# Second layer's gathered experts: the token table in 32 operations, values in two, turned rows and weighing on ScalarE

## What is computed

```python
x_flat = x.reshape(n, c)
scores = (x_flat @ Wg.T).T
top_vals, token_idx = jax.lax.top_k(scores, capacity)
token_w = jax.nn.softmax(top_vals, axis=-1)
xg = x_flat[token_idx]
h = silu(einsum('eic,ehc->eih', xg, W1)) * einsum('eic,ehc->eih', xg, W3)
y = einsum('eih,ech->eic', h, W2) * token_w[..., None]
out = zeros_like(x_flat).at[token_idx.reshape(-1)].add(y.reshape(-1, c))
```

## Time and profile before

| | |
|---|---|
| runs | 2541.8, 2552.1, 2556.6 us |
| profiled execution | 2541.7 us, span 2539.8 |
| busy, share of the span | PE 81%, weight loads 54%, DVE 57%, ACT 42%, POOL 25% |
| the phase of the change | about 1176 to 1336 us of the span |
| its POOL DMAs | 32 gathers 47.4 us busy, 32 scatters 53.5 |
| its tables (`place`) on DVE | 8, together 36.0 us busy |

### The profile page before, as it was taken

One profiled execution on the slowest core, in us unless ns is written; L12 is line 12 of the kernel. 1 busy time (PEld: TensorE's weight loads), 2 busy tenths in 40 slices (PEclk: granted clock), 3 DMA queues, 4 the chain that ended last, 5 costly groups with the idle time before them and its releaser, 6 DMA issues. The chain is left out here.

```text
span 2539.8 us, 42804 instructions
## 1 busy us (share of the span) xinstructions
PE 2055.0 (81%) x16323; PEld 1362.3 (54%) x16323; DVE 1440.6 (57%) x3407; ACT 1068.7 (42%) x2525; POOL 627.8 (25%) x680
## 2 busy tenths in 40 slices
PE   5989999977699993665545678582899999999798
PEld 3546666566566772223324344462566666666565
DVE  2037777534544444555626998014467776777577
ACT  4236556512434442230106534233466666666322
POOL 3018800021200001001674000406233333333100
PEclk9989999978699996675775656695799999999999
DMA  2070110020000003000135001211000000000000
GB/s 60 17 43 5 13 24 2 2 61 16 34 8 1 1 1 116 0 0 9 27 39 176 1 19 35 84 52 50 22 1 1 1 1 1 1 1 1 1 18 17
DMA packets 110168, 61.11 MB, mean 24 GB/s; under 512 B 65272, under 2 KB 104720, under 8 KB 108816
## 3 DMA queue, kind: packets, MB, share of 16 engines
q1 hardware_dynamic: 101568, 49.60, 8.6%
q0 software_dynamic: 7680, 8.40, 1.8%
q10 hardware_dynamic: 720, 0.40, 0.1%
HBM read 36.87 MB, written 21.50 MB: 23 GB/s over the span
## 5 line engine op out<-in xcount | busy, mean ns | idle before, releaser
L2749 ACT ACTIVATE l_prob<-l_ps,l_neg_max 128x128 f32<-128x128 f32 (+1 forms) x512 | 208.2, 419 | 45.6 <-DVE l_neg_max L2809 40.7
L1468 ACT ACTIVATE l0a_prob<-l0a_pst 128x1024 f32<-128x1024 f32 x128 | 131.0, 1024 | 119.9 <-PE l0a_pst L1386 119.9
L2634 POOL TENSOR_TENSOR l_prob<-l_prob,l_total 128x256 f32<-128x256 f32 x128 | 78.4, 612 | 371.9 <-DVE l_total L2817 371.9
L1519 DVE TENSOR_REDUCE l0a_peak<-l0a_ps 128x4 f32<-128x1024 f32 x128 | 156.2, 1221 | 15.8 <-PE l0a_ps L1381 13.7
L2805 DVE TENSOR_TENSOR l_ps<-l_ps,future 128x512 f32<-128x512 f32 x128 | 89.4, 698 | 108.6 <-PE l_ps L2680 108.6
L1381 PE MATMUL l0a_ps<-l0a_k,l0a_q 32*128 32x256 f32 x1024 | 146.3, 405 | 3.3 <-ACT l0a_prob L1468 2.5
L474 ACT ACTIVATE l0e_hidden<-l0e_ph,l0f_b 128x512 f32<-128x512 f32 x128 | 88.0, 687 | 141.1 <-PE l0e_ph L389 141.1
L1386 PE MATMUL l0a_pst<-l0a_q,l0a_k 32*128 32x256 f32 x1024 | 145.8, 400 | 0.2 <-ACT l0a_prob L1468 0.2
L399 PEld LDWEIGHTS l0e_py<-l0f_w,l0e_hidden 128*128 128x128 f32 x1024 | 119.6, 192 | 36.0 <-ACT l0e_hidden L474 32.0
L389 PE MATMUL l0e_ph<-l0f_h_ch,l0f_w 128*128 128x512 f32 x256 | 125.0, 603 | 11.9 <-PEq L43 11.9
L2635 POOL TENSOR_TENSOR l_prob<-l_prob,l_total 128x512 f32<-128x512 f32 x128 | 133.0, 1039 | 0.0
(11 more groups left out here) (481 smaller groups left out, 4949.5 us busy)
## 6 DMA issues: line engine op xcount, KB each, us to landing
l_band<-zero SPq DMA_DIRECT2D x16, 272.0 KB, 3.5
x_tok<-in_x_dram SPq DMA_DIRECT2D x2, 2048.0 KB, 8.0
l2f_w<-in_L_ffn_w_dram SPq DMA_DIRECT2D x2, 2048.0 KB, 9.8
l_rows<-l_band SPq DMA_DIRECT2D x16, 256.0 KB, 3.5
l1f_w<-in_L_ffn_W_dram SPq DMA_DIRECT2D x3, 1024.0 KB, 7.1
gd_tri<-gp_tri SPq DMA_DIRECT2D x8, 256.0 KB, 2.0
l0f_w<-gd_tri SPq DMA_DIRECT2D x8, 256.0 KB, 12.9
gd_tri<-l0f_w SPq DMA_DIRECT2D x8, 256.0 KB, 8.8
```

Source lines behind the costliest of these rows:

```text
L1468: act.activation(prob[:, (n // 2) % 2, pair, :, :].rearrange("p g t s -> p g (t s)"), pst[:, :, :, :].rearrange("p g t s -> p g (t s)"), A ...
L1519: dve.tensor_reduce(to, ps[m % 2][:, :, :, :], AX.X, ALU.max, negate=True).then_inc(max_ready, 1)
L2749: act.activation(prob[:, m % 4, h, cols], ps[m % 2][:, h, cols], ACT.Exp, bias=neg_max[:, m % 4, h, t:t + 1], accum_out=total[:, m % 4, h, ...
```

## The change

The table `place` is made in 32 operations, one for each block, with the lane as a scalar per partition and one streamed input. The five value operations become two, of 2 and 3 values. `save_xt` and `weigh` move from VectorE to ScalarE, the weighing as four operations with the weight as scale. VectorE's order in each turn of the loop becomes `find(e+2)`, both gates, `build(e+3)`; ScalarE's `save_xt(e)`, first Silu, `weigh(e-1)`, second Silu. TensorE, GpSimd and SyncE stay as they are.

```diff
             @block.scalar
             def _(act):
                 act.wait_ge(*ready)
-                for u in range(E * chunks):
+
+                def save_xt(e):
+                    act.wait_ge(turned, e + 1)
+                    if e >= 2:
+                        act.wait_ge(h3_ready, chunks * (e - 1))
+                    act.activation(xt[:, e % 2, :], pt[:, :, :].rearrange("p b t -> p (b t)"), ACT.Copy).then_inc(xt_saved, 1)
+
+                def open_gate(u):
                     act.wait_ge(h1_ready, u + 1)
                     if u >= 2:
                         act.wait_ge(hidden_ready, u - 1)
                     act.activation(act_out[:, u % 2, :], ph1[u % 2][:, :], ACT.Silu).then_inc(act_ready, 1)
+
+                def weigh(e):
+                    act.wait_ge(y_ready, e + 1)
+                    if e >= 2:
+                        act.wait_ge(scattered, 16 * GB * (e - 1))
+                    act.wait_ge(found_ready, e + 1)
+                    for j in range(GB):
+                        ins = act.activation(y[:, e % 2, j, :], py[:, j, :], ACT.Copy, scale=weight[:, e, j:j + 1])
+                    ins.then_inc(y_saved, 1)
+
+                for e in range(E + 1):
+                    if e < E:
+                        save_xt(e)
+                        open_gate(chunks * e)
+                    if e >= 1:
+                        weigh(e - 1)
+                    if e < E:
+                        open_gate(chunks * e + 1)
...
                     link(dve.tensor_tensor(mark[:, e % 2, :, :], r.high[:, e, :].unsqueeze(2).to_broadcast(wide),
                                            r.quarter[:, :].unsqueeze(1).to_broadcast(wide), ALU.is_equal))
-                    for v in range(V):
-                        value = r.number[:, :, v] if v < 2 else r.piece[:, e, :, v - 2]
-                        dve.tensor_tensor(what[:, e % 2, :, :, v], mark[:, e % 2, :, :], value.unsqueeze(2).to_broadcast(wide), ALU.mult)
-                    full = [P, BLK, P]
-                    dve.tensor_tensor(place[:, e % 2, :, :], r.lane[:, e, :].unsqueeze(2).to_broadcast(full),
-                                      r.column[:, :].unsqueeze(1).to_broadcast(full), ALU.is_equal).then_inc(built, 1)
+                    for first, values in ((0, r.number[:, :, :]), (2, r.piece[:, e, :, :])):
+                        n = values.shape[-1]
+                        dve.tensor_tensor(what[:, e % 2, :, :, first:first + n], mark[:, e % 2, :, :].unsqueeze(3).to_broadcast([P, BLK, GB, n]),
+                                          values.unsqueeze(2).to_broadcast([P, BLK, GB, n]), ALU.mult)
+                    for b in range(BLK):
+                        ins = dve.tensor_scalar(place[:, e % 2, b, :], r.column[:, :], r.lane[:, e, b:b + 1], None, ALU.is_equal)
+                    ins.then_inc(built, 1)
...
                 build(0)
                 build(1)
                 find(0)
                 find(1)
                 build(2)
-                for e in range(E + 1):
-                    if e < E:
-                        save_xt(e)
+                for e in range(E):
                     if e + 2 < E:
                         find(e + 2)
-                    if e < E:
-                        gate(chunks * e)
-                    if e >= 1:
-                        weigh(e - 1)
+                    gate(chunks * e)
+                    gate(chunks * e + 1)
                     if e + 3 < E:
                         build(e + 3)
-                    if e < E:
-                        gate(chunks * e + 1)
```

More of the change, by code:

```diff
@@ L2078, in find @@
                        .then_inc(token_ready, 1)
[L2080 to L2084, removed]
                 def gate(u):
@@ L2092, in gate @@
                     dve.tensor_tensor(hidden[:, e % 2, f, :], ph3[u % 2][:, :], act_out[:, u % 2, :], ALU.mult).then_inc(hidden_ready, 1)
[L2094 to L2100, removed]
                 build(0)
```

## The result

The changed kernel took 2554.6 us (median of 16 runs), the kernel before 2548.7 in 16 runs beside it: a ratio of **1.0019, 95% interval 1.0010 to 1.0028**, so 4.8 us slower (0.0019 x 2548.7; the two medians differ by 5.8). The forecast was 2557, 9.3 us over the 2548.0 that it started from, and within 0.5%.

What follows compares the result with a forecast made beforehand. GpSimd's indirect DMAs set the pace, then a VectorE-TensorE loop of 17.3 us per expert against 16.7. Expert 4's scatter +8.9 and weighing +0.4 make +9.3 us on the mean 2548.0: 2557, range 2541 to 2585 (8 in 10).

Steps and rivals of the forecast that it cites:

- The sum: Whole kernel: +8.9 us to expert 4's scatter, +0.4 for weighing after it, +9.3 us in all, 2557 us.
- What bounds: Expert stage: GpSimd's loop, 12.4 us plus some 4 of blocking, and a VectorE-TensorE loop, with little between them.
- The table: VectorE's build: 32 operations 0.205 us apart, 6.6 us in place of 4.4, +2.1 us per build.
- Rival 1: Table at one element per cycle, or value operations as costly as now: +23.9 us, 2572; chance 0.22.
- rival 3: Table's pointer scalar costs nothing: 0.128 us per operation, 19.7 us less, 2537; chance 0.08.
- The values: VectorE's build: two value operations take 1.35 us, giving a build of 8.2 us, now 6.42.
- The loop: VectorE and TensorE per expert: second gate, build, list and projections in a row, 17.3 us where there was 16.7.
- The start: First experts: first gather at about 1195.1, first scatter at about 1229.3 us against 1222.52.
- ScalarE: Moved weighing takes 1.2 us against 0.69, +0.5 only at first and last two scatters; second Silu just hidden.
- Rival 2: GpSimd's indirect DMAs hold VectorE's table operations: five builds by 7.8 us, +39, 2596; chance 0.18 with partial forms.

Runs made afterwards that it cites:

- run 8: Kernel of run 7 with the table in one two-input operation instead of 32; 2540.6 us, stretch (first mark to last expert's first scatter) 137.8 us.
- run 9: Kernel of run 7 with one one-input VectorE operation of 4096 elements, output unread, added to each build; stretch 135.4 us, no time given.
- run 4: Changed kernel with the build of e+3 moved back between the two gates; 2533.5 us in one run, stretch 131.5 us.
- run 7: Changed kernel with TensorE's list of e+2 behind both up-projections and VectorE's finding behind both gates; ratio 0.9896 to the kernel before, stretch 122.1 us.
- run 10: Changed kernel with the values in five operations again, each writing 128 elements side by side, the list's copy turning them; stretch 147.9 us, no time given.
- run 5: Same kernel as run 4, now timed in six executions; ratio 0.9955 to the kernel before, stretch 131.4 us.
- run 1: Kernel before with only the table changed, to 32 operations; 2551.4 us, stretch 150.9 us against 144.0.
- run 2: Kernel before with only the values changed, to two operations; 2542.8 us, stretch 138.5 us against 144.0.
- run 3: Kernel before with only turned rows and weighing moved to ScalarE, build still between the gates; 2547.5 us, stretch 142.2 us against 144.0.
- run 6: Changed kernel with the table in one two-input operation, its order kept; 2545.5 us, stretch 141.4 us.

## Why the prediction was right, and where its terms were off

**The sum.** The forecast loss of 9.3 us is twice the measured one, 4.3 in the trace and 4.8 in the times. What held is the claim of no change beyond 0.5%, 12.7 us, which either loss meets.

**What bounds.** Right: two loops close to each other. GpSimd's blocked instruction is shown by runs 8 and 9, the loop over list and up-projection by runs 4 and 7. A slip: four more instructions of GpSimd are stretched in the kernel before, not five; nothing rests on it.

**The table.** Predicted 0.204 us apart and 6.56 in all; measured 6.26 from the first to the next build's start, 0.196 each. Rival 1 (0.262) and rival 3 (0.128) fall. The rule of the Trainium skill ("VectorE: DVE Perf Modes", section on the TRN2 errata), 122 cycles or 0.127 us, is the shorter by a third; the measured spacing decides. The difference, 0.07, is the one between the trains of before with a pointer scalar and with an immediate (0.131 and 0.061).

**The values.** This term was mis-sized: 1.35 us forecast, 0.85 measured (1178.11 to 1178.96). I had given 0.15 us of each 0.336 to the instruction and the rest to its elements; by the estimate at run 10 some 0.25 is paid once per operation, the step of the output included, and only 0.07 goes to the elements. Eight builds by 0.5 are 4 us: nearly all of the difference between the forecast of 9.3 and the 4.3 of the trace.

**The loop.** 17.3 forecast, 16.2 for the first and 16.9 to 17.0 for the others. Build 7.85 beside GpSimd rather than 8.2, the down-projection 0.2 dearer. GpSimd's idle time ahead of the scatters, 4 to 5 forecast, is 3.8 to 4.6.

**The start.** The first scatter forecast at 1229.3 came at 1226.1: four builds by 0.77 (8.2 - 7.43). The first gather was to come near 1195 and came at 1193.5. A slip: the sum took 3.9 us from the down-projection to the first scatter (1225.4 to 1229.3) and 3.5 to that of expert 4; measured are 3.93 and 3.75.

**ScalarE.** Weighing 1.2 forecast, 1.14; no wait of the second gate for it except in the first expert (1.35 us there). From scatter 4 to scatter 7: 0.4 more forecast, 0.3 measured (32.95 against 32.66).

**Rival 2**, VectorE held by GpSimd: it exists at 0.25 us per build, and not at the 7.8 of its full form. The Trainium skill ("SBUF — State Buffer", section "Who interferes with whom") has the lock for the whole instruction, whoever came first. Run 9 agrees for VectorE first (3.16 us where 1.0 is normal). It does not for an indirect DMA first: the scatter that had begun 1.33 us ahead of the added operation was itself drawn out to 3.69 us while the operation kept its 2.28, and the whole table train grew by 0.3 us beside four DMAs. In the same section a two-input operation is said to stop only what reads SBUF on GpSimd; the scatter of 5.62 us in run 8, which takes its row numbers from SBUF, fits that, though no run here shows that it is this read that was held up.

**The rival that I did not price.** I wrote that the 4 us of blocking "vanish and are worth nothing" in the new order, but not that the order itself was the loss: without it the same change is 0.45% faster (run 5). Every number needed for that stood in the same paragraph: with the build between the gates the sum lacks the 3.8 us from the down-projection to the second gate, which leaves 13.5, and run 4 measured 13.2. Pricing a kernel's parts together hides such a thing; each part should be left out once in the sum.

## What to carry to other kernels

Where two loops over different engines take turns as the bound, take each edit of a change through both, and in the company of the others: here three gain 12.5 us of stretch together and one loses 16.9. Each of the three alone gave 6.8 more (run 1), 5.5 less (run 2) and 1.8 less (run 3), 0.5 less in sum, so single-edit runs did not foretell the 12.5; leaving one edit out did show the loss. Splitting a long VectorE operation into short ones pays when it runs beside GpSimd's indirect DMAs and GpSimd is waited for (15.7 us in run 8), and costs when VectorE's result is waited for (7 us in run 6). A step that only prepares a later round, as the list here, belongs behind the work of this round in an in-order queue, not ahead of it: moving it took the changed kernel from 1.0019 to 0.9896 of the time before.

## What was not expected of the hardware

- VectorE operations pay for a step in a bf16 output (run 10, and the kernels before and after): 128 elements five apart 0.336 us, side by side 0.20, in runs of two and three elements 0.39 and 0.46 for 128 runs.
- The same 16 matmuls of TensorE took 1.79 us at a granted clock of 1.00 and 2.68 at 0.65, in two kernels in which the engine had idled 7 to 8 us shortly before (runs before and 1).
- A one-input VectorE operation of 2.28 us stretched an indirect DMA by 2.1 us, also one that had begun 1.33 us before it; 32 of 0.2 us in a row stretched those beside them by 0.2 at most.
